# An LSTM over graph nodes: node order in memory, and gate products that read their nodes in pairs

## The reference

```python
h = relu(einsum('ts,bsh->bth', adj, x @ Wg0 + bg0))
h = relu(einsum('ts,bsh->bth', adj, h @ Wg1 + bg1))
for p in range(1, 5):
    nw = 1024 // p
    wins = h[:, :nw * p, :].reshape(8 * nw, p, 128)     # windows of p nodes
    last = lstm_last(Wih[p-1], Whh[p-1], bih[p-1], bhh[p-1], wins)
    h = h.at[:, arange(nw) * p + (p - 1), :].set(last)  # last node of each window
out = layernorm(x + h)
```

## Time and profile before

| | us |
|---|---|
| median of 3 runs | 1156.65 |
| lowest, highest | 1156.28, 1158.54 |
| span of the profiled execution | 1154.9 |
| TensorE busy | 1121.8 |
| VectorE busy | 583.2 |
| ScalarE busy | 386.3 |

### The profile page before, as it was taken

The page is one execution under the profiler, slowest core; times in us unless marked ns, Lnnn a source line. Parts: engine busy times, 40 slices in busy tenths (PEclk is TensorE's granted clock), DMA queues, the critical chain, the costliest instruction groups (busy, mean ns, idle before and its releaser), DMA issues.

```text
span 1154.9 us, 15131 instructions
## 1 busy us (share of the span) xinstructions
PE 1121.8 (97%) x5688; PEld 937.5 (81%) x5688; DVE 583.2 (50%) x1426; ACT 386.3 (33%) x696; POOL 0.7 (0%) x6
## 2 busy tenths in 40 slices
PE   6999999999999999999999999999999999999994
PEld 4888988899888988888776878878788787778694
DVE  7233364243442264247646545565655646565667
ACT  6222012120222012133424443444434443435442
POOL 0000000000000000000000000000000000000000
PEclk9999999999999999999999999999999999999997
DMA  9200000000000000012000000000000000000001
GB/s 312 85 1 1 1 1 1 1 1 1 0 0 0 0 0 0 0 39 106 1 1 1 1 1 1 1 19 1 19 1 0 18 0 2 17 19 1 1 19 37
DMA packets 21744, 20.43 MB, mean 18 GB/s; under 512 B 960, under 2 KB 18496, under 8 KB 21696
## 3 DMA queue, kind: packets, MB, share of 16 engines
q1 hardware_dynamic: 21696, 19.81, 5.4%
HBM read 15.61 MB, written 4.19 MB: 17 GB/s over the span
## 4 chain that ended last, share of the span: by engine, by line
PE 94%; DVE 3%; ACT 1%; DMA 0%; issue 0%; ACTq 0%; SPq 0%; DVEq 0%
PE ps L464 27%; PE ps L465 27%; PE ps L466 27%; PE ps L584 8%; PE ps L563 4%; PE ps L566 1%; DVE adj L916 1%; PE ps L755 1%; PE ps L754 0%; DMA xb<-in_x 0%; PE ps L600 0%; DVE square L982 0%; DVE stats L933 0%; DVE node L916 0%; DVE xb L974 0%
## 5 line engine op out<-in xcount | busy, mean ns | idle before, releaser
L861 ACT ACTIVATE gates<-ps,lb 128x256 f32<-128x256 f32 (+2 forms) x273 | 142.6, 567 | 168.1 <-PE ps L466 155.1
L464 PE MATMUL ps<-adj,node 128*128 128x512 f32 x384 | 151.9, 396 | 12.8 <-DVE adj L916 10.1
L465 PE MATMUL ps<-adj,node 128*128 128x512 f32 x384 | 150.3, 391 | 0.0
L466 PE MATMUL ps<-adj,node 128*128 128x512 f32 x384 | 150.3, 391 | 0.0
L801 ACT ACTIVATE y<-ps 128x512 fp32r<-128x512 f32 x48 | 28.7, 598 | 294.5 <-PE ps L466 294.4
L916 DVE TENSOR_TENSOR y<-ps,y 128x512 fp32r<-128x512 f32 x48 | 33.1, 691 | 186.0 <-ACT y L801 186.0
L466 PE MATMUL ps<-ht,lw 128*128 128x256 f32 (+2 forms) x231 | 112.1, 485 | 0.0
L465 PE MATMUL ps<-ht,lw 128*128 128x256 f32 (+2 forms) x231 | 111.9, 485 | 0.0
L464 PE MATMUL ps<-ht,lw 128*128 128x256 f32 (+2 forms) x231 | 111.0, 480 | 0.0
L464 PE MATMUL ps<-adj,h 128*128 128x512 f32 x256 | 99.7, 389 | 0.0
L465 PE MATMUL ps<-adj,h 128*128 128x512 f32 x256 | 99.7, 389 | 0.0
(11 more groups left out here) (167 smaller groups left out, 1975.5 us busy)
## 6 DMA issues: line engine op xcount, KB each, us to landing
square<-in_adj_t SPq DMA_DIRECT2D x8, 512.0 KB, 8.0
xb<-in_x SPq DMA_DIRECT2D x8, 512.0 KB, 7.5
adj_raw<-in_adj_t SPq DMA_DIRECT2D x8, 512.0 KB, 7.7
out<-xb SPq DMA_DIRECT2D x7, 512.0 KB, 3.2
lw_raw<-in_wih_t SPq DMA_DIRECT2D x1, 1024.0 KB, 5.8
lw_raw<-in_whh_t SPq DMA_DIRECT2D x1, 768.0 KB, 7.3
w_raw<-in_w SPq DMA_DIRECT2D x1, 512.0 KB, 11.0
out<-xb SPq DMA_DIRECT2D x2, 256.0 KB, 2.5
```

Source lines behind the costliest of these rows:

```text
L464: pe.matmul(dst, stat(HI), mov(HI), start=start, stop=False)
L465: pe.matmul(dst, stat(HI), mov(LO), start=False, stop=False)
L466: return pe.matmul(dst, stat(LO), mov(HI), start=False, stop=stop)
L861: nc.scalar.activation(gates_in(u.stream)[:, g, at], ps[:, (AHEAD["gate"][slot] + gate) % GB, 0:u.n], ACT.Tanh if g == GG else ACT.Sigmoid ...
```

## The change

x, the rows and columns of adj and the rows of the output are put in another order outside the device. In blocks of 24 nodes, node k and node k+12 lie side by side. 12 is a multiple of 2, 3 and 4, so two neighbours in memory always have the same place in their windows. For the last 16 nodes the distance is 12 for four pairs and 4 for four others. A step s of length p now reads, for each pair of windows, two neighbours: elements 2ps' + 2s and the one behind it, where s' counts pairs of windows. Its moving columns are an access of two dimensions, rows of two elements at a distance of 2p elements, where before they were single elements at a distance of p. The writes to ht go through the same pattern. The stationary reads of ht ("fin") and the p=1 steps read plain rows as before.

For p=3 four tail nodes (1016 to 1019) don't fit the pairs. They lie in ht twice, at their own places and behind the 1024 nodes (four columns, every second one). After the last step of p=2 they are copied behind, and after the last step of p=3 back home: one more VectorE copy of 4 nodes in two parts with a wait ahead of it, and h is released by the copy and no longer by the lo part. p=3 has 344 windows for 342, and ht has 1032 columns for 1026.

```diff
+GROUP = 12
+TAIL_COPY = 8
+TAIL_HOME, TAIL_BEHIND = slice(1017, 1024, 2), slice(1024, 1031, 2)
+def node_order(n):
+    whole = n // (2 * GROUP) * 2 * GROUP
+    order = [v + e * GROUP + k for v in range(0, whole, 2 * GROUP) for k in range(GROUP) for e in range(2)]
+    order += [whole + k + e * GROUP for k in range(4) for e in range(2)]
+    order += [whole + 4 + k + e * 4 for k in range(4) for e in range(2)]
+    assert n - whole == 16 and sorted(order) == list(range(n))
+    return np.asarray(order)
...
-        HTW = N + 2
+        HTW = N + TAIL_COPY
...
+        WINDOWS = {1: BANK, 2: N // 2, 3: (N + TAIL_COPY) // 3, 4: N // 4}
...
+        def moves_tail(u):
+            return u.p in (2, 3) and u.s == u.p - 1
+
+        def cell_steps(u):
+            return (4 if u.s > 0 else 2) + moves_tail(u)
...
-        def columns(u, nw):
-
-            first = u.w0 * u.p + u.s
-            return slice(first, first + u.p * (nw - 1) + 1, u.p)
+        def windows(part, u):
+
+            if u.p == 1:
+                return part[:, u.w0:u.w0 + u.n]
+            return part.rearrange("q (w s e) -> q w s e", s=u.p, e=2)[:, 0:u.n // 2, u.s, :]
...
                             last = product(gate_bank(a), lambda i: lw[:, i, u.p - 1, g * F:(g + 1) * F],
-                                           lambda i: src[:, i, cols], True, u.s == 0)
+                                           lambda i: windows(src[:, i, :], u), True, u.s == 0)
...
+                            dve.wait_ge(tanh_done, ahead("unit", slot, turn, n_ended + 1))
+                            h = in_place(v, GO)
+                            nc.vector.tensor_tensor(h, h, in_place(v, GG), ALU.mult).then_inc(cell_step, 1)
+                            step_reached(n_cell + 1)
+                            if v.s < v.p - 1:
+                                to = hstep_in(v.stream)[:, :, span(v)]
+                                hi, lo = to[:, HI], to[:, LO]
                             else:
...
+                                hi, lo = (windows(h_in(slot, v.back)[:, i, :], v) for i in (HI, LO))
+                                if v.p > 1:
+                                    h = h.rearrange("q (w e) -> q w e", e=2)
+                            nc.vector.tensor_copy(hi, h).then_inc(cell_step, 1)
                             step_reached(n_cell + 2)
-                            lo_part(to[:, LO], h, to[:, HI], h_done)
+                            if moves_tail(v):
+                                lo_part(lo, h, hi, cell_step)
+                                step_reached(n_cell + 3)
+                                both = h_in(slot, v.back)
+                                to, of = (TAIL_BEHIND, TAIL_HOME) if v.p == 2 else (TAIL_HOME, TAIL_BEHIND)
+                                nc.vector.tensor_copy(both[:, :, to], f32(both[:, :, of])).then_inc(h_done, 1)
+                                n_cell += 1
+                            else:
+                                lo_part(lo, h, hi, h_done)
...
+    order = node_order(np.shape(x)[1])
...
-        "x": x, "adj_t": np.asarray(adj).T, "w1": L0_gnn_W1, "w2": L0_gnn_W2, "w3": L0_gnn_W3,
+        "x": np.asarray(x)[:, order], "adj_t": np.asarray(adj).T[order][:, order], "w1": L0_gnn_W1, "w2": L0_gnn_W2, "w3": L0_gnn_W3,
...
-    return r.results[0]["out_0"]
+    return r.results[0]["out_0"][:, np.argsort(order)]
```

More of the change, by code:

```diff
@@ L99, in build @@
         w3s = sb("w3s", [P, K3, 2, F], F32R, w0_at + 8 * (H1 + K2 * H2))
-        lw_raw_at = place(4 * (2 * SKIPS - 1) * G4 + 64)
+        lw_raw_at = place(4 * (2 * SKIPS - 1) * G4 + 128)
         lw_raw = sb("lw_raw", [P, 2 * SKIPS - 1, G4], F32, lw_raw_at)
@@ L110, in build @@
         hstep_last = sb("hstep_last", [P, 2, BANK], F32R, adj_at + 12 * KB + 4 * 5 * BANK)
-        assert gates_at + 4 * 14 * BANK <= lw_raw_at + 4 * (2 * SKIPS - 1) * G4 + 64
+        assert gates_at + 4 * 14 * BANK <= lw_raw_at + 4 * (2 * SKIPS - 1) * G4 + 128
         wg_raw_at = place(2 * KB)
@@ L212, in b_lo_of, with step @@
             return r + 1 + (r >= 6 and splits(slot))
-        Step = namedtuple("Step", "stream p s w0 nw n back held")
+        Step = namedtuple("Step", "stream p s w0 n back held")
+        WINDOWS = {1: BANK, 2: N // 2, 3: (N + TAIL_COPY) // 3, 4: N // 4}
         X, Y, Z = 0, 1, 2
[L220 to L223, removed]
+        def step(stream, p, s, w0=0, back=None, held=False):
+            return Step(stream, p, s, w0, WINDOWS[p], (2 if stream == X else 1) if back is None else back, held)
         def finished_by(item, begun):
@@ L307, in count @@
             return sum(item[0] == name for item in items(slot) if not isinstance(item, Step))
-        CELL_STEPS = (2, 4)
+        def moves_tail(u):
+            return u.p in (2, 3) and u.s == u.p - 1
+        def cell_steps(u):
+            return (4 if u.s > 0 else 2) + moves_tail(u)
         PER_SLOT = {
@@ L315, in build @@
             "unit": lambda n: len(steps_of(n)),
-            "cell": lambda n: sum(CELL_STEPS[u.s > 0] for u in steps_of(n)),
+            "cell": lambda n: sum(cell_steps(u) for u in steps_of(n)),
             "fin": lambda n: count(n, "fin"),
@@ L369, in needs, with span @@
             return before(slot, k, lambda v, b: b + v.back == u.back and (v.p, v.s) == (u.p - 1, u.p - 2))
-        def span(u, n=None):
+        def span(u):
             at = u.w0 % BANK
-            return slice(at, at + (n or u.n))
+            return slice(at, at + u.n)
         def h_in(slot, back):
@@ L637, in pe_slot @@
                             lo_reached(0)
-                        cols = columns(u, u.n)
                         src = h0 if u.p == 1 else h_in(slot, u.back)
@@ L1147, in dve_slot, with in_place @@
                 gate, n_cell, n_fin, n_norm, begun, n_ended = 0, 0, 0, 0, [], 0
-                def in_place(u, g, n=None):
-                    return gates_in(u.stream)[:, g, span(u, n)]
+                def in_place(u, g):
+                    return gates_in(u.stream)[:, g, span(u)]
                 def step_reached(n):
@@ L1176, in dve_slot @@
                         for v in finished_by(u, begun):
-                            if v.s == v.p - 1:
-                                n = v.nw
-                                to = h_in(slot, v.back)[:, :, columns(v, n)]
-                            else:
[L1182 to L1185, removed]
@@ L1186, in dve_slot @@
-                            nc.vector.tensor_tensor(h, h, in_place(v, GG, n), ALU.mult).then_inc(cell_step, 1)
-                            step_reached(n_cell + 1)
-                            nc.vector.tensor_copy(to[:, HI], h).then_inc(cell_step, 1)
-                            step_reached(n_cell + 2)
-                            lo_part(to[:, LO], h, to[:, HI], h_done)
+                            dve.wait_ge(tanh_done, ahead("unit", slot, turn, n_ended + 1))
+                            h = in_place(v, GO)
```

## The result

| | median of runs, us | ratio to the kernel before | 95% interval |
|---|---|---|---|
| forecast | 1054 | 0.911 | |
| kernel before, run beside the changed one | 1156.34 | | |
| changed kernel | 1158.72 | 1.0022 | 1.0015 to 1.0029 |
| the same, a second time | 1158.40 | 1.0023 | 1.0013 to 1.0034 |

The forecast of 1054 us (range 1041 to 1078) was wrong. What happened has the size of the rival "the pairs change nothing" (1157 us), to which I gave 4 in 100.

What follows compares the result with a forecast made beforehand. TensorE was taken to bound the steady slots. 115.2 - 1.5 - 6.4 - 2.3 - 2 + 0.2 - 0.4 = 102.8 us saved, from 1154.9 to 1052.1, plus 1.75 for the runs' median: 1054 us, range 1041 to 1078.

Steps and rivals of the forecast that it cites:

- the pairs change nothing: Rival for the ht reads: the fast way wants a plain row, so 0 saved, 1157 us; chance 0.04.
- What bounds the kernel: Steady slots: TensorE is busy throughout 73.17 us, so time taken from it shortens them; the last stretch follows the LSTM chain.
- Products of ht read pairs: TensorE's ht matmuls for p=2, 3, 4: pairs reach the contiguous pitch, saving 36.6, 37.9 and 40.7, together 115.2 us.
- The weighing of the rule: TensorE's ht reads: the two-hits-per-16-byte-line rule would make p=2 free already; its pitch, 0.452 against 0.234 us, disagrees.
- What is late next: Steady slot, shortened to 58.8 us: cover behind (Y,2,0) falls from 2.7 to 0.07 us; 1.5 us lost over six slots.
- The last slot's waits: Last slot, steps Y and Z alternating: shorter cover makes TensorE wait, and 1.35 us saved buys nothing; 6.4 us lost altogether.
- Clock: Last slot: the lower clock level after waits takes 2.3 us of the saving, and new waits take 2 more.
- Tail move: VectorE's copy behind the last step of p=2 and p=3: 0.2 us, covered in slots, within 0.7 in the last.
- p=3's width: p=3 matmuls with 344 columns instead of 342: 0.4 us lost over eight batches.
- reordering outside: Reordered x, adjacency and output, made outside the device with transfers of the same shapes: cost 0.
- writing h: VectorE's writes of h in pairs: hidden except in the last chain, gain taken as 0.2 us.
- A case with no row behind it: Forecast case for the whole kernel: pairs read at the contiguous pitch, 1054 us, range 1041 to 1078; chance 0.84.

Runs made afterwards that it cites:

- rows_of_4: The changed kernel's whole computation with four neighbours in place of two, read and written in rows of 4: 1050.51 us, 0.9088 of the kernel before.
- rows_of_2_no_gap: The changed kernel with its ht products reading rows of two that follow one another without a gap (wrong nodes): 1049.95 us, ratio 0.9077.

## Why the prediction was wrong

- **What bounds the kernel: right.** TensorE sets the slots. With rows of 4 the products of ht take 113.6 us less in the trace (240.0 to 126.4; the term of the sum was 115.2), and the profiled execution is 106.1 us shorter (1154.9 to 1048.8).
- **"Products of ht read pairs": this step failed.** The bounds were set fairly, 0 and 115.2 us, but I took 115.2 "because the price does not depend on the width of the step", and before it "Pairs would use both" of two elements that a fetch brings. The measured value is 0: 0.452 and 0.232 us for p=2 and p=4, as before, and p=3 1.6 us slower in all. The row of p=2 spoke against it and I misread it. With single columns 2 apart, a line of 16 bytes gives two columns; with pairs, it again gives two. If what counts is how much of a line is used, the pairs of p=2 are the old p=2 in another order. For p=3 and p=4 pairs use more of a line than before, but by the count single columns there were held at the ceiling of 2 cycles, and pairs, at two columns a line, cost just that. Equal prices for steps of 2, 3 and 4 can be a ceiling and need not be a fetch of two.
- **The weighing of the rule: half right.** The Trainium skill (Advanced Engine Details and Errata, section "SBUF Cachelines") says "Need at least two hits on a cacheline to absorb SRAM access latency". Read as "two hits are enough", it is wrong for TensorE here, since it would make the old p=2 (0.452 us against 0.234) and the pairs of the changed kernel free; the trace of before already refuted it. But the 16-byte line that it names is the right unit, and I threw it out with the rule. VectorE's writes agree with the rule: 512 columns with step 2 took 0.69 us in the kernel before (the row below), as in a row (the write of hstep in the earlier trace rows); 256 with step 4 took 620 ns against 426, and in pairs 427.

```profile
840.39 0.69 DVE L916 TENSOR_TENSOR ht<-gates,ht 128x512 fp32r<-128x512 f32 x1
```

- **What is late next: right, as rows_of_4 shows.** A steady slot was to be 58.8 us and is 58.74. The 0.07 us of cover behind (Y,2,0) held: no wait, for which I had put 1.5 us over six slots. The last slot's waits were forecast as 0.8, 1.1, 1.1, 1.3 us and 2.9 us before (Z,3,0); measured are 0.65, 1.25, 0.68, 0.88 and 2.60. The wait before (Z,4,3)'s h grew from 1.65 to 3.01, 1.36 us, which is the 1.35 us that I counted as bought for nothing.
- **Clock: the direction right, the sizes too big.** In rows_of_4 the granted clock is 0.74 of full speed in the nine matmuls of (Z,3,0) behind the wait, and 0.84 in the twelve of (Z,3,1). They take 4.31 us against 6.55 before, so 2.2 of the 3.0 us are saved and 0.8 gone, where I took 2.3. No further drop shows (1.00 from 997.89 to 1027.22, over all four new waits), so the 2 us for it were not needed.
- **The other terms together.** The version whose reads do run at the plain pitch came out at 1050.5 us, 3.5 under the forecast. That is partly luck: the slots (1.5), the clock (1.5 and 2) and the waits (about 1) were put too high by 6 us, but its p=3 is 352 columns wide, which my sum does not have (1.7 us), and about 1 us is not accounted for.
- **Tail move, p=3's width, reordering outside, writing h: small,** as worked out. The copy takes 172 ns (I had 200), and the last wait of TensorE for ht_last is 2.59 us for 2.82, the 0.2 us that I took for writing h. The pitch of p=3, most of the 2 us, was in no term.
- **The chances were wrong more than the sum.** A case with no row behind it got 0.84 and "the pairs change nothing" 0.04, though only the strided end of the bounds had been seen in a row of ht.

## What to carry to other kernels

In this kernel's fp32r matmuls a strided moving operand cost up to twice its time (0.452 against 0.234 us), and what won that back was four neighbours that begin at a multiple of 16 bytes, in every row, part and buffer; two, at the distances of the change (4, 6 and 8), are not half of the gain but none of it. When several patterns cost the same, ask whether that is a ceiling, and count used bytes per line for the new pattern against the old before taking the better bound. An edit whose whole gain hangs on one unmeasured read wants that read measured alone first: a kernel that only reads its columns in pairs would have told it in one run, and one with rows of 4 what to do instead.

## What the runs showed of the hardware that was not expected

- The length of one row of a tile, 1056 or 1058 columns, moves this kernel by 47 us (1050.5 against 1097.9), through the place of its buffers in a line alone.
- Pairs 3 apart are read faster (0.341 us for 512 columns) than pairs 4 apart (0.452), though most of them don't begin at a line.
- A pattern of rows without gaps is folded into a plain one before it reaches the chip (the trace of rows_of_2_no_gap lists one row), so it can't be used to measure short rows.
